# Making the rows of both layer norms on VectorE in place of GpSimd in a transformer block kernel

## The reference

```python
def _layernorm(x, axis=-1, eps=1e-05):
    m = jnp.mean(x, axis=axis, keepdims=True)
    v = jnp.var(x, axis=axis, keepdims=True)
    return (x - m) / jnp.sqrt(v + eps)
...
    h = _L0_tok_ref(x, L0_tok_W)                       # 2304 patches, 768 -> 192
    h = h + _L0_attn_ref(_layernorm(h, axis=-1), ...)  # 12 heads of 16, causal, within an image
    h = h + _L0_ffn_ref(_layernorm(h, axis=-1), ...)   # router, top 2 of 8 experts, 192 -> 768 -> 192, exact gelu
```

## Time and profile before

| what | us |
|---|---|
| three runs: lowest, median, highest | 440.55, 444.43, 451.64 |
| span of the profiled execution | 440.6 |
| TensorE busy in it | 352.8 (80%) |
| VectorE busy | 253.3 (57%) |
| ScalarE busy | 219.6 (50%) |
| GpSimd busy | 196.4 (45%) |

### The profile page before, as it was taken

How to read it: one execution, slowest core, us unless ns; L and a number is a source line. 1 busy time by engine, 2 the same in 40 slices (tenths; PEclk the granted TensorE clock), 3 DMA queues, 4 the chain that set the end, 5 groups by cost and what they waited for, 6 DMA issues and landing times.

```text
span 440.6 us, 14575 instructions
## 1 busy us (share of the span) xinstructions
PE 352.8 (80%) x5602; PEld 327.3 (74%) x5602; DVE 253.3 (57%) x638; ACT 219.6 (50%) x451; POOL 196.4 (45%) x236
## 2 busy tenths in 40 slices
PE   2688879998989989978613189899899898999910
PEld 2687779888989889867512179899899898999810
DVE  2476447787786766774349634455455455355526
ACT  3554647777878787853420034444354344444400
POOL 9005432545745665442630244555555465554210
PEclk9899999999999999995555569999999999999975
DMA  8757000444432333325016021212212122222058
GB/s 306 216 154 224 6 18 19 125 123 123 116 90 78 82 107 111 107 53 158 3 47 168 9 47 49 82 54 86 73 57 82 55 78 69 68 55 49 28 199 312
DMA packets 29386, 42.82 MB, mean 97 GB/s; under 512 B 12352, under 2 KB 18992, under 8 KB 29320
## 3 DMA queue, kind: packets, MB, share of 16 engines
q1 hardware_dynamic: 25192, 33.37, 25.5%
q0 software_dynamic: 4128, 8.50, 6.7%
HBM read 30.23 MB, written 9.67 MB: 91 GB/s over the span
## 4 chain that ended last, share of the span: by engine, by line
PE 48%; issue 14%; DVE 13%; POOL 10%; ACT 8%; DMA 5%; SPq 1%; POOLq 0%; ACTq 0%; DVEq 0%
PE PSA L1185 19%; PE PSA L1200 13%; PE PSA L966 5%; POOL XF L446 3%; POOL YP L458 2%; DMA W2h<-yrows 2%; DMA W2l<-wqkv 2%; PE PSA L1023 2%; PE PSA L1204 2%; PE PSA L1152 2%; DVE REG L660 2%; DVE PTR L888 1%; PE PSA L998 1%; PE PSA L1049 1%; POOL REG L453 1%
## 5 line engine op out<-in xcount | busy, mean ns | idle before, releaser
L646 ACT ACTIVATE PTR<-PSA 128x768 f32<-128x768 f32 x43 | 34.8, 810 | 100.9 <-PE PSA L1185 74.7
L1185 PE MATMUL PSA<-YT,W1h 128*128 128x128 f16 x774 | 80.0, 222 | 5.7 <-issue 3.6
L1185 PE MATMUL PSA<-YT,W1l 128*128 128x128 f16 (+1 forms) x516 | 77.2, 223 | 0.0
L1185 PEld LDWEIGHTS PSA<-YT,W1h 128*128 x774 | 65.1, 99 | 10.1 <-issue 5.5
L490 POOL DMA_INDIRECT yrows<-KBR x43 | 43.0, 1000 | 65.8 <-DVE KBR L932 65.5
L1200 PE MATMUL PSA<-W2h,PTR 128*128 x516 | 71.0, 246 | 0.3 <-DVE PTR L660 0.3
L485 POOL DMA_INDIRECT REG<-xrows,KBR x43 | 45.5, 1057 | 42.9 <-DVE KBR L909 25.3
L1200 PE MATMUL PSA<-W2l,PTR 128*128 x258 | 63.5, 246 | 0.0
L660 DVE SCALAR_TENSOR_TENSOR PTR<-PTR 128x768 f16<-128x768 f32 x43 | 41.2, 958 | 33.7 <-ACT PTR L651 27.2
L966 PE MATMUL PSA<-W2h,REG 128*108 128x192 f16 x396 | 39.4, 261 | 17.7 <-DVE REG L660 17.2
L966 PEld LDWEIGHTS PSA<-W2h,REG 128*108 128x108 f16 x396 | 36.2, 137 | 20.3 <-DVE REG L660 11.5
(11 more groups left out here) (163 smaller groups left out, 789.7 us busy)
## 6 DMA issues: line engine op xcount, KB each, us to landing
WSTG<-w SPq DMA_DIRECT2D x16, 384.0 KB, 3.7
WSTG<-w SPq DMA_DIRECT2D x16, 336.0 KB, 3.2
REG<-xt SPq DMA_DIRECT2D x12, 324.0 KB, 4.6
W1l<-xt SPq DMA_DIRECT2D x10, 324.0 KB, 3.4
VB<-VP SPq DMA_DIRECT2D x99, 19.1 KB
H<-hrows SPq DMA_DIRECT2D x6, 288.0 KB
xrows<-REG SPq DMA_DIRECT2D x1, 1600.5 KB
hrows<-H SPq DMA_DIRECT2D x1, 1296.0 KB
```

What stands on the lines that cost most here:

```text
L646: nc.scalar.activation(g.rearrange("p (h c) -> p h c", h=2), PSA[:, 2 * u * 512:(2 * u + 2) * 512].rearrange("p (h c) -> p h c", h=2)[:, : ...
L1185: ins = nc.tensor.matmul(bank(2 * u + f // (FC // 2), 128, FC // 2 * ST_)[:, w:w + ST_], weights[a, c], YT[0:rows, at:at + ST_], start=k = ...
```

## The change

The functions that make a norm's row (subtract the mean, multiply by the inverse deviation, float32) leave GpSimd's stream and enter VectorE's, with the same operands and the same waits. On GpSimd they stood at the end of its loop body, behind `y_low`; on VectorE they stand at the end of its `step`, behind `probs_lo` and the group's `refine`. 22 rows of each norm are moved; nothing else is.

```diff
@@ gpsimd
-            def norm1_row(t):
-                need(gp, rs_done, 1 if t < FIRST_NORM else 2)
-                need(gp, n1_lo, t - 1)
-                nc.gpsimd.tensor_scalar(two(XF[0], t, C), htile(t), MEAN[:, t:t + 1], RS[:, t:t + 1],
-                                        ALU.subtract, ALU.mult).then_inc(n1_row, 1)
...
-            def norm2_row(t):
-                need(gp, rs_done, group(t) + 1)
-                need(gp, n2_lo, 2 * t - 2)
-                nc.gpsimd.tensor_scalar(two(XF[1], t, C), htile(t), MEAN[:, NT + t:NT + t + 1], RS[:, NT + t:NT + t + 1],
-                                        ALU.subtract, ALU.mult).then_inc(n2_row, 1)
...
                 if has(i - 1):
                     y_low(i - 1)
-                if has(i + 6):
-                    norm1_row(i + 6)
-                for t in norm2_at(i):
-                    norm2_row(t)
@@ vector
+            def norm1_row(t):
+                need(dve, rs_done, 1 if t < FIRST_NORM else 2)
+                need(dve, n1_lo, t - 1)
+                nc.vector.tensor_scalar(two(XF[0], t, C), htile(t), MEAN[:, t:t + 1], RS[:, t:t + 1],
+                                        ALU.subtract, ALU.mult).then_inc(n1_row, 1)
+
+            def norm2_row(t):
+                need(dve, rs_done, group(t) + 1)
+                need(dve, n2_lo, 2 * t - 2)
+                nc.vector.tensor_scalar(two(XF[1], t, C), htile(t), MEAN[:, NT + t:NT + t + 1], RS[:, NT + t:NT + t + 1],
+                                        ALU.subtract, ALU.mult).then_inc(n2_row, 1)
...
                 if group_end(i - 2):
                     refine(group(i - 2))
+                if has(i + 6):
+                    norm1_row(i + 6)
+                for t in norm2_at(i):
+                    norm2_row(t)
```

## The result

The changed kernel took 442.18 us (median of 20 runs, 439.1 to 454.69), the kernel before, on the same chip, 444.6 (20 runs, 440.55 to 457.35). The ratio of the two is 0.9944, with a 95% interval of 0.9916 to 0.9972: 2.5 us less, between 1.2 and 3.7. The medians are of all runs; each ratio here leaves out the slow runs of both kernels, those more than 1.5% above the fastest of the same kernel. The forecast was 442.2 and 2.2 us less.

A forecast was written before the change was run, and what follows sets the result against it. TensorE was taken to bound the steady attention stretch (86.93 of 94 us busy). Terms 1.01 - 0.98 + 2.13 gave 2.2 us less, taking the median from 444.43 to 442.2 us; range 437.5 to 449.0.

The forecast's parts named there:

- The row's price: Each moved row on VectorE: 0.35 us long, taking 0.27 us of the engine's time, from the nearest comparable row.
- D: Rival: rows of 1.01 us make VectorE the bound; 13.5 us slower, 458; chance 0.04.
- B: Rival: a row on VectorE takes only 0.25 us, 0.17 of engine time; 3.0 us gained, 441.4; chance 0.17.
- Plain steps: 0: Steady attention steps: VectorE's idle 0.61 us covers two rows needing 0.54, so nothing is gained or lost.
- Group steps: 1.0 gained: Steps 6, 10, 14, 18, after a group's inverse deviation: TensorE starts earlier, 0.34 + 0.34 + 0.15 + 0.18 = 1.01 us.
- rival A: Attention's low part on GpSimd held by both weight pieces also in steps 6 and 10; 1.2 us gained, 443.2; chance 0.23.
- Start: 1.0 lost: First tiles, rows behind other VectorE work: tile 0 gains 0.35; tiles 3 to 6 lose 0.39, 0.40, 0.27, 0.27 us.
- End: 2.1 gained: Last three steps, where nothing hides the rows: waits of 0.69 and 0.23 go, last transposes 1.21 earlier; 2.13 us.
- Sum: Whole kernel: group steps, start and end together give 2.2 us less, median 442.2 us.
- C, the clock: Rival: new gaps at the start make TensorE's clock fall early; with two steps 5.0 us slower, 449.4; chance 0.11.

The follow-up runs named there:

- e8: Changed kernel plus two spare rows, read by nobody, at the end of each of VectorE's 22 tile steps: 446.63 us, ratio 1.0073 to the kernel before.
- e1: The changed kernel run again without any edit, for a second profile: 441.85 us, ratio 0.9952 to the kernel before.
- e2: Against the kernel before, only the second norm's rows on VectorE, the first norm's left on GpSimd: 444.08 us, ratio 0.9972.
- e4: Against the kernel before, only the first norm's rows moved to VectorE: 445.46 us, ratio 1.0025.
- e3: Against the kernel before, only the second norm's rows of the last six tiles on VectorE: 444.07 us, ratio 0.994.
- e7: Kernel before, all rows still on GpSimd, with the second norm's row, high and low parts ahead of the first's: 445.68 us, ratio 1.0028.
- e9: Changed kernel with the weight pieces' low parts moved to the end of VectorE's step, behind the rows: 445.93 us, ratio 1.0023 to the kernel before.
- e10: Changed kernel with the weight pieces' low parts last on VectorE and the second norm ahead of the first: 442.51 us, ratio 0.9976 to the kernel before.
- e6: Changed kernel with the second norm ahead of the first on VectorE, ScalarE and GpSimd: 449.1 us, ratio 1.0133 to the kernel before.
- e12: Kernel before, all rows on GpSimd, with the weight pieces' low parts at the end of VectorE's step: 458.64 us in six runs, no ratio.

## Why the prediction was right

**The row's price.** 0.37 and 0.29 us against 0.35 and 0.27. D is out by a factor of 2.7, and B too: nothing of 0.25 us is seen. The Trainium skill, VectorE: DVE Perf Modes, "Mode 2×_2P", has two results a cycle for this form, 0.26 us as an estimate from that page; the measured 0.37 differs, and decides.

**Plain steps: 0.** Right (6.31 in all three profiles). e8 shows that the margin was larger than the 0.07 us that I read off the tightest step: two rows more are still hidden in the plain steps.

**Group steps: 1.0 gained.** The sum was near, by luck in part, its parts less so. At full clock the steps 6, 10, 14 and 18 of e1 are 0.25, 0.32, 0.45 and 0.13 shorter (1.15; forecast 0.34, 0.34, 0.15, 0.18), step 7 is 0.13 longer and step 9 0.22 shorter. Two errors stand against each other. One is the attention's low part: I had it clear of the pieces in steps 6 and 10, but in e1 it takes 1.38, 1.37, 1.34 and 1.34 us in steps 6, 10, 14 and 18 (rival A's mechanism; its price is a part of A's, as TensorE waits 0.15 us for it in steps 6 and 10 and 0.37 in step 18). Only in step 10 of the first profile was it clear. The other is a gain that I did not see. TensorE's wait for the second norm fell by 0.67 in step 10, where the row is 0.30 of it, and by 0.61 in step 14, where 0.34 was forecast (in step 18 by 0.70, of 0.73 forecast). VectorE's small instructions of the variance had been held off by GpSimd; before, step 10:

```profile
123.33 0.20 DVE L688 TENSOR_SCALAR MEAN<-MEAN 108x4 f32<-108x4 f32 x1
123.45 0.32 DVE L689 SCALAR_TENSOR_TENSOR DM<-DM 108x4 f32<-108x4 f32 x1
123.80 0.16 DVE L691 TENSOR_TENSOR VAR<-VAR,DM 108x4 f32<-108x4 f32 x1
124.00 0.29 DVE L693 TENSOR_SCALAR HV<-VAR 108x4 f32<-108x4 f32 x1
...
123.26 1.01 POOL L435 TENSOR_SCALAR XF<-H,MEAN,RS 108x192 f32<-108x192 f32 x1
```

and after, with no row on GpSimd:

```profile
123.31 0.17 DVE L672 TENSOR_SCALAR MEAN<-MEAN 108x4 f32<-108x4 f32 x1
123.39 0.16 DVE L673 SCALAR_TENSOR_TENSOR DM<-DM 108x4 f32<-108x4 f32 x1
123.58 0.17 DVE L675 TENSOR_TENSOR VAR<-VAR,DM 108x4 f32<-108x4 f32 x1
123.78 0.17 DVE L677 TENSOR_SCALAR HV<-VAR 108x4 f32<-108x4 f32 x1
```

From the statistics to the first piece it is 1.72 us (122.14 to 123.86) instead of 1.92 (122.16 to 124.08). The cause is the first norm's row on GpSimd: in e2, which keeps it there, the four instructions take 0.20, 0.32, 0.16 and 0.29 again, and in e4, which moves it alone, 0.17, 0.15, 0.17 and 0.17. Step 9 has its part from the same row: before, L435 took 1.71 us there beside VectorE's pieces (from 117.10 us), and TensorE waited 0.14 for L453; that wait is gone in e1, e2 and e4. A few tenths of the shorter waits were not traced.

**Start: 1.0 lost.** The step that failed is "the row delays the statistics of the whole first norm by 0.27" (tile 5) and its twin for tile 6. Tiles 3 and 4 cost 0.41 and 0.42 (0.39 and 0.40), and the wait ahead of the patches at 38 us fell from 1.09 to 0.76, the 0.33 of tile 0 (0.35). Tiles 5 and 6 cost nothing: from the value's low part to the first shift it is 2.19 us (61.03 to 63.22), with a row of 0.29 in it, against 2.21 (61.84 to 64.05) without, and step 0 is 5.43 against 5.45. Part of the cause is the same as above: before, L685 took 0.54 there and the refinement's L703 0.41, beside GpSimd; after, their likes take 0.17. So the start lost 0.5, not 1.0.

**End: 2.1 gained.** 0.69 and 0.23 are gone, and the last part is 1.18 (2.98 less 1.80) against 1.21. e3 shows it alone (2.1 us from the last scores to the last transposes). Behind the last transposes nothing changed: 217.4 us to the end before, 217.3 and 217.0 in the two profiles of the changed kernel.

**Sum.** 0.5 lost, 1.2 and 2.1 gained are 2.8 by the steps at full clock; the runs say 2.5 (1.2 to 3.7) and 2.1 (0.5 to 3.7) as they came, and 2.9 +- 0.6 at equal clock. The 2.2 forecast is about half a microsecond short of its own parts, for the most part by the two rows at the start that were priced at 0.27 each and cost nothing. That the median came out at 442.18 against 442.2 is luck: the median moves with the clocks of the runs by more than that.

**C, the clock.** Dips between 60 and 190 us came in the first profile of the changed kernel, in e4's, in the second one of the kernel before and in e7's (all rows on GpSimd), and not in e1's or the first of before. So they need no change of the rows.

## What to carry to other kernels

Price an operation by the nearest row of the same engine and the same tile, and look then at its place in the new engine's queue: the rows' move was worth 2 to 3 us, after its place in the queue at the start had taken 0.85. Ask also whom the removed instructions were holding off: it showed here as one short instruction with two lengths. Moving a long holder elsewhere moved its price to whoever stood there (e9), and turning the order with it undid that (e10). And set every kernel against the unchanged one on the same chip: the unchanged kernel differed by 1.6 us between chips at an equal clock, which is as much as most effects here.

## What the runs showed beyond what was expected

- VectorE's instructions with two operands in SBUF and GpSimd's hold each other off in both directions, down to instructions of four columns: 0.16 became 0.32, and at 14 columns 0.17 became 0.54, on VectorE; GpSimd's 0.55 became 1.37 and 1.95, its row of 1.0 became 1.64. The Trainium skill, SBUF — State Buffer, "Who interferes with whom", has the exclusion, and these rows agree. VectorE's instructions that read one tensor only are held as well: L693 took 0.29 instead of 0.17 beside L435, and the row 0.68 and 0.69 instead of 0.37 beside L441 in e2; the same section has it for this operation where it uses both ports.
- The clock has a life of its own: of 82 runs of the kernel before, taken beside the experiments, 23 had a mean clock under 0.885, of 32 of the changed kernel 2, of e10's twelve none, of e6's six 5 and of e12's six 4. So the kernel seems to shift how often the clock dips. No run here tells by what.
